# Attention of a four-block model on one core: VectorE's takings placed behind TensorE's products, a second pair of part buffers, another order of the DMA queue, and narrow key blocks in one step

## The reference

```python
x = x + _layernorm(_L0_attn_ref(_layernorm(x), Wq, bq, Wk, bk, Wv, bv, Wo, bo))

q = (x @ Wq.T + bq).reshape(b, l, h, hd).transpose(0, 2, 1, 3)   # k, v likewise
scores = jnp.einsum('bhqd,bhkd->bhqk', q, k) / math.sqrt(hd)
scores = jnp.where(causal, scores, -jnp.inf)
att = jax.nn.softmax(scores, axis=-1)
out = jnp.einsum('bhqk,bhkd->bhqd', att, v).transpose(0, 2, 1, 3).reshape(b, l, d)
return out @ Wo.T + bo
```

## Time and profile before

| | us |
|---|---|
| median of 3 runs | 4374.48 (4363.74 to 4383.02) |
| the profiled execution's own time | 4376.63 |
| its span | 4374.9 |
| attention, prologue, first batch row | 29.2 to 131.3 |
| attention, from the first score to the end, first batch row | 131.3 to 483.5 |
| TensorE busy | 3951.7 (90%) |
| VectorE busy | 2711.7 (62%) |
| ScalarE busy | 1695.0 (39%) |
| GpSimd busy | 1819.8 (42%) |

### The profile page before, as it was taken

How to read it: one execution, slowest core, us unless ns; L and a number is a source line. 1 busy time by engine, 2 the same in 40 slices (tenths; PEclk the granted TensorE clock), 3 DMA queues, 4 the chain that set the end, 5 groups by cost and what they waited for, 6 DMA issues and landing times.

```text
span 4374.9 us, 61678 instructions
## 1 busy us (share of the span) xinstructions
PE 3951.7 (90%) x18308; PEld 2853.3 (65%) x18308; DVE 2711.7 (62%) x5034; ACT 1695.0 (39%) x3538; POOL 1819.8 (42%) x1951
## 2 busy tenths in 40 slices
PE   7899799779999999979778997997899999999797
PEld 5444477557777777757654444775577777777576
DVE  3557344567777777764435574445677777777644
ACT  1334411245555555542113344112455555555411
POOL 1111332345565665544311113323455556555543
PEclk8677899899999999989976778998999999999899
DMA  3221011011000110001132210110110001100011
GB/s 71 35 35 31 28 44 36 19 37 32 23 26 29 34 31 26 24 15 44 38 75 35 35 31 28 44 36 19 37 32 25 24 29 34 31 27 23 15 45 40
DMA packets 80974, 145.13 MB, mean 33 GB/s; under 512 B 16152, under 2 KB 18056, under 8 KB 80784
## 3 DMA queue, kind: packets, MB, share of 16 engines
q1 hardware_dynamic: 80784, 142.84, 12.4%
HBM read 112.64 MB, written 4.19 MB: 27 GB/s over the span
## 4 chain that ended last, share of the span: by engine, by line
PE 71%; issue 11%; DVE 7%; ACT 4%; POOL 2%; DVEq 2%; POOLq 1%; SPq 1%; DMA 1%; ACTq 0%
PE banks L485 15%; PE banks L486 14%; PE banks L487 14%; PE banks L826 4%; PE banks L665 4%; PE banks L646 3%; PE banks L622 3%; PE banks L819 2%; PE banks L839 2%; DVE conv L1338 2%; PE banks L529 2%; DVEq L1341 1%; PE banks L761 1%; PE banks L762 1%; POOL X L1503 1%
## 5 line engine op out<-in xcount | busy, mean ns | idle before, releaser
L1338 DVE SCALAR_TENSOR_TENSOR conv<-banks,cpar,conv 128x509 f32<-128x509 f32 (+2 forms) x576 | 428.2, 744 | 115.9 <-ACT conv L999 101.5
L1166 DVE TENSOR_TENSOR Y<-banks,Y 128x512 f32<-128x512 f32 x400 | 275.6, 691 | 233.5 <-PE banks L487 233.2
L942 ACT ACTIVATE probs<-banks 128x1024 f32<-128x1024 f32 (+3 forms) x384 | 298.1, 809 | 310.4 <-PE banks L646 309.5
L622 PE MATMUL banks<-stack_k,stack_q 48*128 48x512 f32 (+3 forms) x768 | 335.9, 510 | 58.8 <-DVEq L1212 19.6
L1573 POOL TENSOR_SCALAR_AFFINE_SELECT probs<-probs 128x256 f32<-128x256 f32 x256 | 104.2, 408 | 663.2 <-ACT probs L942 662.9
L1637 POOL TENSOR_TENSOR state<-state,gt 128x512 f32<-128x512 f32 x112 | 133.5, 1192 | 499.5 <-PE banks L819 499.5
L1484 POOL TENSOR_SCALAR f_hi<-f_raw 128x512 fp32r<-128x512 f32 x150 | 93.8, 625 | 581.4 <-PE banks L487 472.7
L485 PE MATMUL banks<-xhi,f_hi 128*128 128x512 f32 x800 | 328.5, 411 | 3.5 <-DVE xlo L1137 3.5
L485 PE MATMUL banks<-xhi,wx_hi 128*128 128x512 f32 x768 | 312.6, 407 | 15.9 <-DVE conv L1338 15.9
L486 PE MATMUL banks<-xhi,f_lo 128*128 128x512 f32 x800 | 319.9, 400 | 0.0
L487 PE MATMUL banks<-xlo,f_hi 128*128 128x512 f32 x800 | 319.5, 399 | 0.0
(11 more groups left out here) (203 smaller groups left out, 10353.5 us busy)
## 6 DMA issues: line engine op xcount, KB each, us to landing
m_raw<-in_w_mamba SPq DMA_DIRECT2D x224, 256.0 KB, 2.6
f_raw<-in_w_ffn SPq DMA_DIRECT2D x50, 768.0 KB, 4.6
stack_q<-part_hi SPq DMA_DIRECT2D x128, 64.0 KB, 2.4
stack_k<-part_hi SPq DMA_DIRECT2D x128, 64.0 KB, 2.5
X<-in_x SPq DMA_DIRECT2D x4, 1024.0 KB, 6.6
wqk_raw<-in_w_attn SPq DMA_DIRECT2D x8, 512.0 KB, 3.5
stack_q<-part_lo SPq DMA_DIRECT2D x64, 64.0 KB, 2.4
stack_k<-part_lo SPq DMA_DIRECT2D x64, 64.0 KB, 2.5
```

Of the source, the lines that this page charges most:

```text
L622: r = pe.matmul(dst[:, 0:cols], stack_q[buf][base:base + ROWS, h, i * P:(i + 1) * P], stack_k[buf][base:base + ROWS, h, s * HALF:s * HALF ...
L942: act.activation(probs[n % 2][:, 2 * p:2 * p + 2, 0:w], banks[:, 2 * p:2 * p + 2, 0:w], ACT.Exp, scale=1.0 / HD ** 0.5).then_inc(exp_done[ ...
L1166: dve.tensor_tensor(Y[:, i, :], bank[6 + i % 2], Y[:, i, :], ALU.add).then_inc(f["dn_used"], 1)
L1338: r = dve.scalar_tensor_tensor(out=rest, in0=src[:, 0:HALF - lag], scalar=cpar[:, o:o + 1], in1=rest, op0=ALU.mult, op1=ALU.add)
```

## The change

In the list, what TensorE makes and what VectorE takes become separate entries (`values_out`, `turn_out`, `maxima_out`, `proj_hi`, `proj_lo`), which may stand later.

- **Prologue.** Two values_in instead of five stand ahead of the pieces, and the other six among them. `values_out` stands five pieces behind its product. Of f = 1 only the uses 0 and 1 are made in the prologue. The ring may use seven banks there (4, 5, 7 and the still empty 0 to 3).
- **The ring.** The bank of each use is worked out in `ring_banks()`: the one that is freed earliest. TensorE waits for exactly the entry that freed it. From the first score on there are three banks, as before.
- **Projections in the quads.** A use is cut into two halves of 6 matmuls, placed behind two successive steps (`PROJ_STEPS`), and VectorE's part comes two steps after the second half began. f = 1, uses 2 and 3, stand in quad 0; f = 2 from quad 0 to quad 1; f = 3 in quads 2 and 3.
- **Turns.** `turn` stands one step later or earlier (after steps 2 and 6), and `turn_out` a step behind it.
- **Steps.** The last two blocks of each half, 256 and 128 wide, are one step of 384. There are 10 steps in a quad.
- **Part buffers.** `part_hi` and `part_lo` get a second buffer each, in the memory of `X`. `X` is therefore loaded from HBM again at the end of the attention phase, once all stacks have landed, and GpSimd's residual add waits for that.
- **DMA queue.** A piece waits for the six DMAs of its own head, not for 24. The weights of f = 1 are loaded ahead of the first stacks. `put_maxima(1)` stands ahead of `stack(3)` (before: behind it), and from there on one stack and one `put_maxima` alternate.

```diff
-                part_hi = sb("part_hi", [P, 2, L], F32R, stack=s2)
-                part_lo = sb("part_lo", [P, 2, L], F32R, stack=s2)
+                part_hi = [sb("part_hi", [P, 2, L], F32R, stack=s2)[:]]
+                part_lo = [sb("part_lo", [P, 2, L], F32R, stack=s2)[:]]
+                for part, h in ((part_hi, 0), (part_lo, 1)):
+                    own = X[:, h * CPH:(h + 1) * CPH, :].rearrange("p (w u) d -> p w (u d)", w=2)
+                    part.append(own.bitcast(F32R))
...
-        STEPS = [(s, j) for s in range(2) for j in range(CPH * (s + 1))]
+        STEPS = [(s, (j,) if j < CPH * (s + 1) - 2 else (j, j + 1)) for s in range(2) for j in range(CPH * (s + 1) - 1)]
...
+        MAIN_BANKS, FIRST_BANKS = (4, 5, 7), (4, 5, 7, 0, 1, 2, 3)
+
+        PROJ_STEPS = {}
+        for f, use, t, n in ((1, 2, 0, 0), (1, 3, 0, 2), (2, 0, 0, 6), (2, 1, 1, 0), (2, 2, 1, 3), (2, 3, 1, 6),
+                             (3, 0, 2, 2), (3, 1, 2, 6), (3, 2, 3, 0), (3, 3, 3, 4)):
+            PROJ_STEPS[t, n], PROJ_STEPS[t, n + 1] = (f, use, 0), (f, use, 1)
...
+            for n in range(NP):
+                if n % 6 == 3 and n < 36:
+                    yield "values_in", 2 + n // 6
+                if n % 6 == 2 and 2 < n < 42:
+                    yield "values_out", 1 + n // 6
...
-                        for _ in range(0 if turning else 2 if n in (2, 3) and q == 0 else 1):
-                            if pieces:
-                                yield "piece", *pieces.pop(0)
+                        turning = n == NS - 2 and q < 2 and t + 1 < NQ
+                        more = n < NS - 2 and q == 0 or n in (0, 4) and q == 2
+                        yield from some(0 if turning else 2 if more else 1)
+                        if n == NS - 2 and q == 2 and t + 1 < NQ:
+                            yield "maxima_out", t + 1
+                        if q == 1 and n == 3 and t > 0:
+                            yield "turn_out", t - 1, 1
...
+                        if q == 2 and (t, n - 2) in PROJ_STEPS and PROJ_STEPS[t, n - 2][2]:
+                            yield "proj_lo", *PROJ_STEPS[t, n - 2][:2]
...
+        def ring_banks():
+
+            last, bank_of, before = {}, {}, {}
+            for use in RING_USES:
+                started_at = ORDER.index(use)
+                main = started_at >= ORDER.index(("score", 0, 0, 0))
+                allowed = MAIN_BANKS if main else FIRST_BANKS
+                k = min(allowed, key=lambda i: (last[i][2] if i in last else -1))
+                bank_of[use[:3]], before[use[:3]] = k, last.get(k)
+                last[k] = release(use)
+                if not main:
+                    first_scores = dict(last)
+            return bank_of, before, first_scores
...
+                for t in range(2, NQ):
+                    if t + 1 < NQ:
+                        stack(t + 1)
...
+                load_x(b)
```

More of the change, by code:

```diff
@@ L295, in attention_order @@
+                if n == 45:
+                    yield "proj_lo", 1, 0
+                yield from some(1)
+            yield "maxima", 0
+            yield from some(2)
+            yield "maxima_out", 0
+            yield from some(2)
+            yield "proj_lo", 1, 1
+            yield from some(AHEAD - 4)
             for t in range(NQ):
@@ L314, in attention_order @@
                 yield "values", t, NS - 1
             yield "turn", NQ - 1, 1
+            yield "turn_out", NQ - 1, 1
         ORDER = list(attention_order())
+        RING_USES = [o for o in ORDER if o[0] in ("piece", "values_in", "maxima", "turn") or o[0] == "proj" and o[3] == 0]
+        RING_ENDS = [o[:3] for o in ORDER if o[0] in ("piece", "values_in", "maxima", "turn") or o[0] == "proj" and o[3]]
+        RING = len(RING_ENDS)
+        FREED = {"piece": "piece", "values_in": "values_out", "turn": "turn_out"}
@@ new lines, in build, with release @@
+        FREES = [o for o in ORDER if o[0] in FREED.values()]
+        FREE = len(FREES)
+        def release(use):
+            kind, *arg = use
+            if kind == "proj":
+                return "part_lo_ready", 4 * arg[0] + arg[1] + 1, ORDER.index(("proj_lo", *arg[:2]))
+            if kind == "maxima":
+                return "mt_ready", arg[0] + 1, ORDER.index(("maxima_out", *arg))
+            end = (FREED[kind], *arg)
+            return "ring_free", FREES.index(end) + 1, ORDER.index(end)
```

289 lines of the change are left out of this document (146 added, 143 removed).

## The result

| | before | after |
|---|---|---|
| median, us | 4378.17 (4 runs, 4363.74 to 4383.02) | 4483.24 (4 runs, 4480.75 to 4484.16) |
| ratio | | 1.0245, 95% interval 1.0219 to 1.027 |
| span of the profiled execution | 4374.9 | 4482.4 |
| TensorE busy | 3951.7 | 4031.5 |

The change makes the kernel 105 us slower. The prediction was 4244, with 0.05 on slower.

What follows compares the result with a forecast made beforehand. The prediction took TensorE to bound the quads, losing its granted clock, and in the prologue also waits. Prologue and quads, doubled for two batch rows: 4376.6 - 2 x (37.5 + 29) = 4244 us, range 4105 to 4325.

Steps and rivals of the forecast that it cites:

- The prologue, -37.5: Before the first score: pieces start at 50.0, first score at 93.5 instead of 131.3, saving 37.5 us a batch row.
- The quads, -29: Attention quads: fewer stalls, merging and a higher clock save 18, 8 and 3 us, together 29 a batch row.
- 0.80 for the first stage (from 0.69) and 0.78 for the second (from 0.74): TensorE's granted clock, forecast to rise in the earlier quads (first stage) and the later quads with pieces (second).
- TensorE at 93 to 94% of its clock: Quads: share of its granted clock that TensorE fills with work, 91 to 92% before, with VectorE next in line.
- In the quads with pieces TensorE covers it: Merging the 256 and 128 wide blocks: no gain in quads with pieces, some 3 us in the last quad.
- While a projection or a turn holds one of the three banks, pieces have two: Ring in the quads: a drawback named beside the removed projection stalls, with no size given.
- the 13 us a row of the sum: TensorE's stalls at the quads' 8 projections a batch row, 1.6 us each, counted as removed.
- The 4 us, twice, for GpSimd's split: Quads: TensorE waits about 4 us, twice, for GpSimd's split behind the masks; f = 3 remains, so 5 us stay.
- At nothing: Second load of X, covered by the last quad, and the moved `put_maxima(1)`, covered except up to 4 us at full clock.
- Case 2: Rival: the clock in the quads stays as it is, so only the prologue gains; 4312 us, chance 0.22.
- Case 3: Rival: without idle gaps the clock stays up in all of the quads; 4113 us, chance 0.15.
- Case 4: Rival: slower; pieces on two banks stall TensorE and the clock falls for good; 4568 us at 0.50 throughout, chance 0.05.

Runs made afterwards that it cites:

- e4_old_loop: The change's prologue, banks, part buffers, DMA queue and second load of X, with the loop of the kernel before; 4313 us, ratio 0.9854 to the kernel before.
- e3: The change with each projection use of the quads as twelve matmuls in one step instead of two halves; 4447 us.
- e7: e4_old_loop with the quads' projections cut into two halves in successive steps, taken at once behind the second; 4319 us.
- e10: e4_old_loop with the low part of each projection in the quads taken two steps later; 4291 us.
- e13: e4_old_loop with projections in halves and their low parts taken two steps behind the second half; 4355 us.
- e5: e4_old_loop with the 10 merged steps and the piece pairs that they need; 4356 us.
- e11: e4_old_loop with the turn of a quad's second half in step 2 instead of step 1, taken at once; 4331 us.
- e14: e4_old_loop with merged steps and piece pairs, the turn in step 2, and turns taken a step late; 4401 us.
- e8: The change with four 128x512 products added ahead of each turn in quads 4 to 7, 64 in all; 4447 us.

## Why the prediction was wrong

- **The prologue, -37.5: right.** First piece at 51.2 for 50.0, first score at 95.45 for 93.5: -35.9. The clock was 0.90 for the 0.85 taken; VectorE was busy for 32.90 of 44.20 us, 74% and not above 80, and one wait of 4 us stayed. In e4_old_loop the first score is at 92.3, and the term stands by itself: -39 a row, of which quad 7 takes 11 back.
- **The quads, -29: this step failed**, with +89 in its place. It failed in two of its factors. "I take 0.80 for the first stage (from 0.69) and 0.78 for the second (from 0.74)": measured 0.67 and 0.54, in the second row 0.64 and 0.64. "TensorE at 93 to 94% of its clock": 77% in quads 0 to 3, worked out under e3. For quads 0 to 3 the forecast gives 134.4 / (0.80 x 0.93) = 181 us, the measured clock alone 134.4 / (0.67 x 0.93) = 216, and 260.4 were measured: 35 us by the clock and 45 by the other factor. In quads 4 to 6, 109 were forecast and 144.4 measured, all by the clock.
- *Why the clock was mis-sized.* The prediction read that busy time alone doesn't bring the clock back, and then took the stalls' end and the halves as reasons for a rise. The halves do nothing for the clock (e7: 0.79 in quads 0 to 3, as e4). And it costed two edits at nothing that do: merging ("In the quads with pieces TensorE covers it") costs 43 us, and the turn's new step, not costed at all, 17. That a stretch of scores, pieces and values alone stands at 0.50 was in the earlier trace rows; that a merged step makes such rows longer was not asked.
- *Why the waits were mis-sized.* "While a projection or a turn holds one of the three banks, pieces have two" stood there without a price. With ten uses of two and a half steps each this is 25 of the 40 steps of quads 0 to 3, and the turns beside. The lost stalls were real but half as large as the 13 us a row of the sum. The chain from the last matmul to the freed bank is 1.6 us, but TensorE still has scores and two pieces to make in it and stands only at the third: 6.3 us in eight waits. The 4 us, twice, for GpSimd's split are mis-sized too: TensorE waits 3.5 us for `wqk_lo` in two waits there, and 2.6 in the change, for the 5 of the sum. e10, which has the late takings alone, has 3.4 us less a row in quads 0 to 3. Halves and late takings together cost 23 a row (e13).
- **"At nothing": right.** The load of X, the second buffers and the queue cost nothing that is seen (e4). The score's wait for `mt_lo` is 2.9 us, inside the 4 allowed.
- **The rivals.** Case 2, the clock as it was, 4312: this is where e4 stands, 4313, with the old order, but by luck. Its clock in quads 4 to 6 is the old one (0.75 for 0.74); in quads 0 to 3, which have two uses more, it is 0.79 for 0.70, and quad 7 takes 23 us more. Case 3, the clock stays up: refuted. The Trainium skill, TensorE: Matmul & The Clock Gate, "Why this matters for your kernels", asks for a busy TensorE without longer gaps to keep the clock; here it was busy for 96% of 144 us with no wait above 0.5 us, and had 0.54. Case 4, slower, was the outcome, with both of its pieces: two banks for pieces, and the clock down. Its bound held: slower from a mean clock below 0.64 in the quads, and (260.4 x 0.67 + 144.4 x 0.54 + 36.8 x 0.63) / 441.6 is 0.62. Its mechanism was half right. It let the clock fall because TensorE waits, but in quads 4 to 6 TensorE hardly waits (4.5 us before pieces in 144.4); there the clock fell with the merged steps and the turns (e5, e11, e14), in one row further than in the other. 0.05 was far too little: the stretch in the earlier trace rows was evidence for it.

## What to carry to other kernels

Where the granted clock is what a stage loses, ask of each edit how it changes the order of the work on TensorE, and not only what wait it ends: merging steps was to end waits, and it cost 43 us with almost none added. That this is because the turns and products of 128 rows then lie further apart fits e5, e8 and e11, and is not shown by itself. A taking that is put off spares its own engine a wait and costs the ring a bank for as long; multiply the steps by the uses before calling it free. Read both batch rows before giving a stage a price: the same list differed by 12 us between them. And split a change: its prologue and buffers with the old loop gain 59 us, and the order of its loop cost 170.

## What was unexpected of the hardware

- Added work made a kernel faster: 64 matmuls of 128x512 more, some 30 us less (e8), with a clock of 0.73 for 0.54 in quads 4 to 6 of the first row and 0.73 for 0.64 in the second.
- TensorE was busy for 18.10 of 18.30 us and stayed at the lower level; its busy share doesn't tell here which level it gets.
- One list of instructions, twice in one execution: quads 4 to 6 of the change take 144.4 us at 0.54 and then 132.5 at 0.64.
- The same code of quad 7 takes 25.0 us at 0.93 or 36.3 us at 0.55, in most kernels the same in both rows, and other kernels with the same code in it have the other. Two kernels can so differ by 20 us for an edit that stands elsewhere.
